# Graph attention followed by a tree of feed-forward nodes: attention weights that leave PSUM once as fp32, in place of two 16-bit halves

## What is computed

```
q = layernorm(x) @ Wq.T + bq            # 512 tokens, 8 heads x 16
k = (h_neigh + E[adj]) @ Wk.T + bk      # 512 neighbours
v = (h_neigh + E[adj]) @ Wv.T + bv
scores = einsum('bhd,bnhd->bhn', q, k) / 4
scores = where(adj == 0, -1e9, scores)
attn   = softmax(scores); attn = where(adj == 0, 0, attn)
x = x + einsum('bhn,bnhd->bhd', attn, v) @ Wo.T + bo
x = x + tree_ffn(layernorm(x))          # 8 levels, 255 nodes
```

## Time and profile before

| what | value |
|---|---|
| median of three runs | 167.42 us |
| profiled execution, first to last instruction | 165.2 us |
| TensorE matmul busy (PE) | 101.6 us, 829 records |
| TensorE weight load busy (PEld) | 77.8 us, 830 records |
| VectorE busy (DVE) | 112.1 us |
| ScalarE busy (ACT) | 69.9 us |
| GpSimd busy (POOL) | 43.1 us |

### The profile page before, as it was taken

How to read it: one execution, slowest core, us unless ns; L and a number is a source line. 1 busy time by engine, 2 the same in 40 slices (tenths; PEclk the granted TensorE clock), 3 DMA queues, 4 the chain that set the end, 5 groups by cost and what they waited for, 6 DMA issues and landing times.

```text
span 165.2 us, 3073 instructions
## 1 busy us (share of the span) xinstructions
PE 101.6 (62%) x829; PEld 77.8 (47%) x830; DVE 112.1 (68%) x302; ACT 69.9 (42%) x167; POOL 43.1 (26%) x82
## 2 busy tenths in 40 slices
PE   0675007943878777865615444978888838688820
PEld 0161003833745555544504233537787738588720
DVE  0596904881699999996587689843645695846571
ACT  3232204890789989987100000335434322413420
POOL 2332920000000000000064000543443533754652
PEclk9999999997899999999755555599999999959996
DMA  5927640224999999999320000010000000000000
GB/s 155 306 81 207 115 105 25 50 74 141 383 405 446 421 440 436 412 442 406 156 65 0 0 4 0 16 48 0 0 4 4 0 2 0 16 16 0 0 6 26
DMA packets 6341, 22.35 MB, mean 135 GB/s; under 512 B 1755, under 2 KB 4826, under 8 KB 5722
## 3 DMA queue, kind: packets, MB, share of 16 engines
q1 hardware_dynamic: 4970, 20.78, 33.3%
q10 hardware_dynamic: 1104, 0.92, 1.8%
q0 software_dynamic: 256, 0.52, 1.1%
HBM read 20.91 MB, written 1.31 MB: 135 GB/s over the span
## 4 chain that ended last, share of the span: by engine, by line
PE 37%; DVE 17%; DMA 13%; issue 12%; ACT 9%; SPq 6%; POOL 2%; DVEq 1%; ACTq 0%; POOLq 0%
PE s_ps L641 11%; DMA early<-q_parts 7%; SPq L248 6%; PE turn_ps L641 4%; ACT prob L395 4%; PE turn_ps L512 3%; DVE prob L751 3%; ACT prob_t L391 3%; DVE row_pair L682 2%; DMA w_sb<-in_w_t 2%; PE aux_ps L641 2%; PE s_ps L566 2%; PE s_ps L539 2%; DMA q_parts<-q_p 2%; PE misc_ps L641 2%
## 5 line engine op out<-in xcount | busy, mean ns | idle before, releaser
L512 PE MATMUL turn_ps<-ident,prob 128*128 128x128 f32 x128 | 23.0, 309 | 8.0 <-ACT prob L395 6.6
L395 ACT ACTIVATE prob<-prob,negmax 128x512 f32<-128x512 f32 x32 | 23.0, 720 | 11.1 <-DVE negmax L751 11.0
L751 DVE CUSTOM_DVE_ANT_0 prob<-s_ps,mask 128x512 f32<-128x512 f32 x32 | 21.7, 682 | 8.5 <-PE s_ps L481 8.4
L353 POOL TENSOR_TENSOR early<-early,scaled_sb 128x128 f32<-128x128 f32 x48 | 20.5, 454 | 26.5 <-ACT scaled_sb L437 25.8
L758 DVE TENSOR_TENSOR prob_t<-turn_ps,prob_t 128x512 f16<-128x512 f32 x32 | 22.1, 689 | 6.2 <-ACT prob_t L391 6.2
L641 PE MATMUL s_ps<-w,msg 128*128 x128 | 19.2, 295 | 8.3 <-issue 4.5
L512 PEld LDWEIGHTS turn_ps<-ident,prob 128*128 128x128 f32 x128 | 15.8, 156 | 16.3 <-ACT prob L395 15.5
L481 PE MATMUL s_ps<-early 96*128 96x512 bf16 x32 | 13.7, 436 | 15.1 <-DMA early<-q_parts 14.2
L641 PEld LDWEIGHTS s_ps<-w,msg 128*128 128x128 f32 x128 | 16.3, 200 | 10.8 <-issue 10.7
L391 ACT ACTIVATE prob_t<-turn_ps 128x512 f16<-128x512 f32 x32 | 18.6, 580 | 6.6 <-PE s_ps L491 6.1
L437 ACT ACTIVATE scaled_sb<-s_ps,coef 128x128 f32<-128x128 f32 x32 | 10.0, 363 | 21.2 <-PE s_ps L641 21.2
(11 more groups left out here) (147 smaller groups left out, 163.8 us busy)
## 6 DMA issues: line engine op xcount, KB each, us to landing
w<-in_w_t SPq DMA_DIRECT2D x3, 4096.0 KB, 23.2
w<-in_w_t SPq DMA_DIRECT2D x1, 4032.0 KB, 41.6
prob<-in_adj SPq DMA_DIRECT2D x1, 1024.0 KB, 8.8
k_parts<-early SPq DMA_DIRECT2D x1, 384.0 KB, 2.5
early<-k_parts SPq DMA_DIRECT2D x1, 384.0 KB, 4.5
q_parts<-q_p SPq DMA_DIRECT2D x1, 288.0 KB, 3.4
early<-q_parts SPq DMA_DIRECT2D x1, 288.0 KB
msg<-in_neigh_t SPq DMA_DIRECT2D x1, 256.0 KB, 2.8
```

The costliest lines, as they stand in the source:

```text
L353: ins = nc.gpsimd.tensor_tensor(mine, mine, scaled_sb[:, i, :], ALU.add)
L395: nc.scalar.activation(prob[:, u % RING, :], prob[:, u % RING, :], ACT.Exp, bias=negmax[:, t, h:h + 1], scale=-1.0, accum_out=psums[:, t, ...
L512: last = nc.tensor.transpose(turn_ps[u % 2][:, m * P:(m + 1) * P], prob[:, u % RING, m * P:(m + 1) * P], ident[:])
L751: nc.vector.tensor_tensor_reduce(out=prob[:, u % RING, :], in0=score_ps[u % 2], in1=mask[:, t, :], scale=1.0, scalar=3.0e38, op0=ALU.add, ...
```

## The change

Five things change.

1. `prob_t` is fp32, with one copy of each unit's weights in place of two fp16 halves, in a ring of three (`TURNED`).
2. Even units are copied from PSUM by ScalarE, odd units by VectorE (`tensor_copy`); the subtraction L758 is gone.
3. `weighted_values` is 4 matmuls with fp32 operands, in place of 8 with 16-bit ones. The moving operand is 17 columns: 16 channels and a column of ones, whose product is the row sum.
4. `exp` no longer accumulates the row sum. The sum comes out of column 16 of `o_raw`, to which VectorE copies a tile's output (in place of the reduction L763). The reciprocal now waits for the last tile's copy.
5. The values are no longer split: VectorE writes them straight to `v_st`, GpSimd sets the column of ones. Three activations of ScalarE and two subtractions of GpSimd in the head go.

The core of the diff:

```diff
-        v_st = sb("v_st", [P, NT, HEADS, PARTS, DH], BF16)
+        v_st = sb("v_st", [P, NT, HEADS, DH + 1])
-        prob_t = sb("prob_t", [P, 2, 2, N_NEIGH], F16)
+        prob_t = sb("prob_t", [P, TURNED, N_NEIGH])
...
-            for i in range(PARTS - 1):
-                pool.wait_ge(v_split, 2 * i + 2)
-                nc.gpsimd.tensor_tensor(v_f.rearrange("p (a c) -> p a c", c=DH),
...
+            nc.gpsimd.memset(v_st[:, :, :, DH:DH + 1], 1.0).then_inc(v_ready, 1)
...
             for u in range(UNITS + LAG):
-                if u >= LAG:
+                if u >= LAG and (u - LAG) % 2 == 0:
                     v = u - LAG
                     act.wait_ge(turned, v + 1)
-                    if v >= 2:
-                        act.wait_ge(summed, v - 1)
-                    nc.scalar.activation(prob_t[:, v % 2, 0, :], turn_ps[v % 2][:], ACT.Copy).then_inc(hi_moved, 1)
+                    if v >= TURNED:
+                        act.wait_ge(summed, v - TURNED + 1)
+                    nc.scalar.activation(prob_t[:, v % TURNED, :], turn_ps[v % 2][:], ACT.Copy).then_inc(moved[0], 1)
...
                     nc.scalar.activation(prob[:, u % RING, :], prob[:, u % RING, :], ACT.Exp,
-                                         bias=negmax[:, t, h:h + 1], scale=-1.0,
-                                         accum_out=psums[:, t, h:h + 1]).then_inc(exped, 1)
+                                         bias=negmax[:, t, h:h + 1], scale=-1.0).then_inc(exped, 1)
...
             def weighted_values(u):
                 t, h = divmod(u, HEADS)
-                pe.wait_ge(lo_moved, u + 1)
+                pe.wait_ge(moved[u % 2], u // 2 + 1)
...
-                for i in range(2):
-                    for m in range(NT):
-                        last = nc.tensor.matmul(o_ps[t % 2][:, h * PARTS * DH:(h + 1) * PARTS * DH],
-                                                prob_t[:, u % 2, i, m * P:(m + 1) * P],
-                                                v_st[:, m, h].rearrange("p i c -> p (i c)"),
-                                                start=(i == 0 and m == 0), stop=(i == 1 and m == NT - 1))
+                for m in range(NT):
+                    last = nc.tensor.matmul(o_ps[t % 2][:, h * (DH + 1):(h + 1) * (DH + 1)],
+                                            prob_t[:, u % TURNED, m * P:(m + 1) * P], v_st[:, m, h, :],
+                                            start=(m == 0), stop=(m == NT - 1))
...
-                if u >= LAG:
+                if u >= LAG and (u - LAG) % 2 == 1:
                     v = u - LAG
-                    dve.wait_ge(hi_moved, v + 1)
-                    nc.vector.tensor_tensor(prob_t[:, v % 2, 1, :], turn_ps[v % 2][:], prob_t[:, v % 2, 0, :],
-                                            ALU.subtract).then_inc(lo_moved, 1)
+                    dve.wait_ge(turned, v + 1)
+                    if v >= TURNED:
+                        dve.wait_ge(summed, v - TURNED + 1)
+                    nc.vector.tensor_copy(prob_t[:, v % TURNED, :], turn_ps[v % 2][:]).then_inc(moved[1], 1)
...
-                    nc.vector.tensor_reduce(o_sb[:, t, :].rearrange("p (h c) -> p h c", c=DH),
-                                            o_ps[t % 2].rearrange("p (h i c) -> p h c i", i=PARTS, c=DH),
-                                            AX_X, ALU.add).then_inc(o_moved, 1)
+                    nc.vector.tensor_copy(o_raw[:, t].rearrange("p h c -> p (h c)"), o_ps[t % 2]
+                                          ).then_inc(o_moved, 1)
...
-            dve.wait_ge(exped, UNITS)
             dve.wait_ge(masked, UNITS)
-            nc.vector.reciprocal(psums[:], psums[:]).then_inc(live_ready, 1)
+            dve.wait_ge(o_moved, TILES)
+            nc.vector.reciprocal(rsums[:], o_raw[:, :, :, DH]).then_inc(live_ready, 1)
```

More of the change, by code:

```diff
@@ L32 @@
 RING = 4
+TURNED = 3
 W2_PARTS = 4
@@ L166, in gnn_ffn_kernel @@
         adj_sb = prob[:].bitcast(I32)
-        k_f, q_f, v_f = o_t[:], x1[:].rearrange("p t d -> p (t d)"), o_sb[:].rearrange("p t d -> p (t d)")
+        k_f, q_f = o_t[:], x1[:].rearrange("p t d -> p (t d)")
         perm = view(prob[:], 0, TILES * N_TOK, F16, "p (t s) -> p t s", s=N_TOK)
@@ L185, in gnn_ffn_kernel @@
         score_ps = [s_ps[:, i, :] for i in range(2)]
-        o_ps = [s_ps[:, 2 + i, 0:HEADS * PARTS * DH] for i in range(2)]
+        o_ps = [s_ps[:, 2 + i, 0:HEADS * (DH + 1)] for i in range(2)]
         turn_ps = [ps(f"turn_ps{i}") for i in range(2)]
@@ L203, in gnn_ffn_kernel @@
             sem("veps_ready"), sem("rstd_ready"), sem("h_ready"), sem("ht_ready"))
-        x_biased, k_split, v_split = sem("x_biased"), sem("k_split"), sem("v_split")
+        x_biased, k_split, v_ready = sem("x_biased"), sem("k_split"), sem("v_ready")
         q_split, q_done, q_out, q_stacked = (
@@ L208, in gnn_ffn_kernel @@
         k_out, k_stacked = sem("k_out"), sem("k_stacked")
-        scored, masked, exped, turned, hi_moved, lo_moved, summed = (
-            sem("scored"), sem("masked"), sem("exped"), sem("turned"), sem("hi_moved"), sem("lo_moved"),
-            sem("summed"))
+        scored, masked, exped, turned, summed = (
+            sem("scored"), sem("masked"), sem("exped"), sem("turned"), sem("summed"))
+        moved = [sem("moved_by_act"), sem("moved_by_dve")]
         o_moved = sem("o_moved")
@@ L329, in _ @@
             pool.wait_ge(summed, UNITS)
-            pool.wait_ge(lo_moved, UNITS)
+            for i in range(2):
+                pool.wait_ge(moved[i], UNITS // 2)
             for i in range(len(Q_SLICES)):
@@ L505, in _ @@
                 if u >= 2:
-                    pe.wait_ge(lo_moved, u - 1)
+                    pe.wait_ge(moved[u % 2], u // 2)
                 if u == 0:
-                    pe.wait_ge(v_split, 1)
+                    pe.wait_ge(v_ready, 2)
                 if u == 1:
@@ L514, in _ @@
                 last.then_inc(turned, 1)
-                if u == LAG:
-                    pe.wait_ge(v_split, 2 * PARTS)
                 if u >= LAG:
@@ L735, in _ @@
             dve.wait_ge(row_in, 16)
[L736 to L739, removed]
+            nc.vector.tensor_tensor(v_st[:, :, :, 0:DH],
+                                    turn_ps[0][:].rearrange("p (m h c) -> p m h c", h=HEADS, c=DH),
+                                    row_sb[:, BV:BV + D].rearrange("p (h c) -> p h c", c=DH).unsqueeze(1
+                                                                   ).to_broadcast([P, NT, HEADS, DH]), ALU.add
+                                    ).then_inc(v_ready, 1)
             query_parts(1)
@@ L762, in _ @@
                     dve.wait_ge(summed, HEADS * (t + 1))
-                    nc.vector.tensor_reduce(o_sb[:, t, :].rearrange("p (h c) -> p h c", c=DH),
-                                            o_ps[t % 2].rearrange("p (h i c) -> p h c i", i=PARTS, c=DH),
-                                            AX_X, ALU.add).then_inc(o_moved, 1)
-            dve.wait_ge(exped, UNITS)
+                    nc.vector.tensor_copy(o_raw[:, t].rearrange("p h c -> p (h c)"), o_ps[t % 2]
+                                          ).then_inc(o_moved, 1)
             dve.wait_ge(masked, UNITS)
-            nc.vector.reciprocal(psums[:], psums[:]).then_inc(live_ready, 1)
+            dve.wait_ge(o_moved, TILES)
+            nc.vector.reciprocal(rsums[:], o_raw[:, :, :, DH]).then_inc(live_ready, 1)
             nc.vector.tensor_scalar(live[:], negmax[:], 0.5 * MASKED, None, ALU.is_lt).then_inc(live_ready, 1)
             dve.wait_ge(live_ready, 2)
-            then(nc.vector.tensor_tensor(live[:], live[:], psums[:], ALU.mult))
-            dve.wait_ge(o_moved, TILES)
-            by_head = o_sb[:].rearrange("p t (h c) -> p (t h) c", c=DH)
-            scale = live[:].rearrange("p t h -> p (t h)").unsqueeze(2)
+            then(nc.vector.tensor_tensor(live[:], live[:], rsums[:], ALU.mult))
+            by_head = o_sb[:].rearrange("p t (h c) -> p t h c", c=DH)
             for t0, t1 in GROUPS:
-                part = by_head[:, t0 * HEADS:t1 * HEADS, :]
-                nc.vector.tensor_tensor(part, part, scale[:, t0 * HEADS:t1 * HEADS, :].to_broadcast(
-                    [P, (t1 - t0) * HEADS, DH]), ALU.mult).then_inc(o_ready, 1)
+                nc.vector.tensor_tensor(by_head[:, t0:t1], o_raw[:, t0:t1, :, 0:DH],
+                                        live[:, t0:t1, :].unsqueeze(3).to_broadcast([P, t1 - t0, HEADS, DH]),
+                                        ALU.mult).then_inc(o_ready, 1)
             dve.wait_ge(x_biased, 1)
```

12 lines of the change are left out of this document (3 added, 9 removed).

## The result

| | before | changed |
|---|---|---|
| median (runs) | 167.8 us (4) | 206.3 us (4), 205.6 to 207.5 |
| ratio | | 1.2285, 95% interval 1.2226 to 1.2344 |
| span of the profiled execution | 165.2 us | 203.8 us |
| PE / PEld busy | 101.6 / 77.8 us | 147.8 / 127.2 us |
| DVE / ACT busy | 112.1 / 69.9 us | 103.9 / 58.3 us |

The forecast was 170.4 us, with a range of 168.2 to 174.0. The sign was right and the size was far off: +38.5 us where +3.0 was forecast. In what follows a median is over all executions of a kernel, while a ratio leaves out its slow ones (over 1.5% above its fastest), so it can differ from the ratio of two medians.

A forecast was written before the change was run, and what follows sets the result against it. VectorE and ScalarE set the pace before; TensorE was to become the bound. Its 40.6 us from 39.88 end the loop 2.4 us later, small waits add 0.6: 167.4 + 3.0 = 170.4 us, range 168.2 to 174.0.

The forecast's parts named there:

- TensorE becomes the bound: Loop: fp32 values matmuls fill TensorE, 0.81 us a group, 1.45 us a round, above 1.03 for VectorE and ScalarE.
- At half clock for the first 3.05 us, of which half is lost: 1.5: Loop from 39.88 us: TensorE starts at half clock for 3.05 us, adding 1.5 us to its 40.6 us sum.
- the clock doesn't fall at 39.5: Rival, pause ahead of unit 8: added groups shorten the pause, 1.5 us aren't lost, 168.9 us; chance 12%.
- Ahead of 39.88 nothing changes: Head, before unit 8's scores: the stage still ends at 39.88 us, dropped value parts and added groups being hidden.
- The head's slack of 5.8 us for the added groups: Ahead of 39.88 us: TensorE's 5.8 us idle hides four costlier weighted-value groups, 3.2 to 5.4 us.
- VectorE's copy: 0.69 us: Loop, every second unit: VectorE's plain copy of a 128x512 fp32 bank costs 0.69 us at the upper end.
- The elementwise round: Loop: were VectorE and ScalarE still the bound, a round would be about 1.03 us.
- Behind the loop: After the last weighted values: a shorter copy replaces the reduction but its wait precedes the reciprocal; no change, -0.3 to +0.3 us.

The follow-up runs named there:

- kernels with a filler: Changed kernel plus unused matmuls ahead of unit 8's scores: 12, 206.6 and 175.5 us; 20, 176.6 us; 20 with GpSimd's constants after the eighth mask step, 169.7 to 176.4.
- the run with late constants: Changed kernel with GpSimd's constants (memsets, iotas) started only after the eighth mask step: 204.7 us (204.1 to 205.3).

## Why the prediction was wrong, step by step

- **TensorE becomes the bound, each fp32 product being two loads and two matmuls, 0.112 us a record: right.** The groups stand as 256 records. At full clock the eight of a unit take 0.82 us (forecast 0.81), a round is 1.47 us (1.45), and the loop takes 39.8 us (39.7).
- **"At half clock for the first 3.05 us, of which half is lost: 1.5": this step failed.** It took the time at half clock from the kernel before and put it under other rounds. The time at half was 109 us, 76 of them the loop. At 2.80 in place of 1.47 us the 26 rounds lose 34.6 us where the term had 1.5: 33 of the 35.5 us of the miss. The rows to doubt it with were there: before, the clock came back at 42.93 after rounds of which the values took 0.21 us of 0.86; I had just worked out that in the new round 0.81 of 1.45 us is spent loading, and didn't ask whether such rounds would win the clock back. I weighed a clock rival of one sign only, the one that doesn't fall. What the chip takes for work that raises the clock stays open.
- **The rival "the clock doesn't fall at 39.5"** named the place that matters and had the price wrong: it was to be worth 1.5 us, and by the kernels with a filler it is worth some 30. Its condition failed too: TensorE stopped at 37.07 us, hardly later than before (36.90), since the added groups fitted into its idle time, and the pause grew to 5.1 us. By their times no execution of the changed kernel had it.
- **"Ahead of 39.88 nothing changes": failed, by 2.3 us**, of which the run with late constants gives back 1.6. The value parts dropped from GpSimd were hidden themselves, but GpSimd's next instructions moved up by 6 us onto VectorE's cast, which is on the way to the query slices. I counted what was removed and not what moved into its place.
- **The head's slack of 5.8 us for the added groups: right in effect.** TensorE was idle from 37.1 us on, and the transfer still decided.
- **VectorE's copy: 0.69 us, right** (0.692). The elementwise round: 1.03 forecast, 0.98 measured with the 16-bit operands.
- **Behind the loop: right within bounds.** From the last values to the scaling VectorE takes 118.92 - 117.87 = 1.05 us, before 1.12.

```profile
117.87 0.30 DVE L754 COPY o_raw<-s_ps 128x136 f32<-128x136 f32 x1 [4.24 <-PE s_ps L483]
118.27 0.35 DVE L760 RECIPROCAL rsums<-o_raw 128x32 f32<-128x32 f32 x1
...
118.92 0.76 DVE L766 TENSOR_TENSOR row_pair<-o_raw,live 128x256 f32<-128x256 f32 x2
```

## What to carry to other kernels

Where TensorE becomes the bound, price its round at both clocks, and ask of each round whether it would win the clock back once it is at half; a round that is mostly weight loads beside short matmuls may not, and then the clock at the loop's start sets the pace of the whole loop. A matmul with few columns costs its load: an fp32 product here is two loads, and each load with its matmul steps 0.112 us against 0.026 for a 16-bit one, so the two 16-bit halves were the cheaper way for TensorE (0.21 against 0.82 us a unit). When work is taken off an engine that is off the path, look at what moves up into its place and whom that meets.

## What was not expected of the hardware

- With TensorE's records covering the whole of 42.16 to 117.83 us and its loads 94% of that, the granted clock stayed at 0.50. The Trainium skill (TensorE: Matmul & The Clock Gate, Part 1) says that the clock is gated down by default and that activity releases it; this trace doesn't agree if loads, and matmuls that wait for their loads, are taken for activity, and no run here shows how they are taken. Rounds with the same loads and 64 columns in place of 17 brought it back in 7.1 us.
- The same rounds kept a full clock for 41 us once they had it (two profiles). What keeps the clock up is not enough to bring it back.
- An fp32 weight load steps 0.112 us at full clock and 0.213 at half, so it follows TensorE's clock; with 17 or with 64 columns streamed beside it the group of eight takes 0.82 and 0.84 us at full clock.
- The clock ahead of the pause differs from one execution to the next: the same first rounds stood at 1.00 from 31.4 us in one profile and at 0.50 until 46.9 in another. This would explain why the kernels with a filler show two times, 170 and 176 us, though none of the 170s was profiled. Open is what decides it, and why in one execution of five of the kernel with three unused matmuls a round the clock fell at 40.9 us and stayed at half.
